# A six-sublayer decoder: order of the start, strips, experts by halves of ranks, and DVE stages as single operations

## What is computed

```
x = LN(x + attention with relative positions(x))      # a: 16 heads of 8
x = LN(x + cross attention(x, ctx))                    # b: 16 heads of 64
x = LN(x + experts(x))                                 # m, c: 7 experts of 256 slots and one that passes on
x = LN(x + gated linear attention with decay(x))       # d: 16 heads, rank 16, a norm of its own inside
x = LN(x + cross attention(x, ctx))                    # e: 16 heads of 8
x = LN(x + quantised feed-forward with a convolution(x))  # f: 512 wide, ternary weights
```

## Time and profile before

| | us |
|---|---|
| median of 3 runs | 922.15 |
| lowest and highest | 916.98, 922.53 |
| the profiled execution | 916.87 |
| its span | 915.1 |
| round of the first loop | 26.45 |
| round of the second loop | 19.59 |

### The profile page before, as it was taken

How to read it: one execution, slowest core, us unless ns; L and a number is a source line. 1 busy time by engine, 2 the same in 40 slices (tenths; PEclk the granted TensorE clock), 3 DMA queues, 4 the chain that set the end, 5 groups by cost and what they waited for, 6 DMA issues and landing times.

```text
span 915.1 us, 21252 instructions
## 1 busy us (share of the span) xinstructions
PE 753.2 (82%) x8906; PEld 552.4 (60%) x8906; DVE 565.2 (62%) x1520; ACT 402.5 (44%) x1026; POOL 215.2 (24%) x215
## 2 busy tenths in 40 slices
PE   3679999999999799999876675789888888988874
PEld 2346666767666577666665473666666665766541
DVE  0046665556666766666663733687788887788722
ACT  1345444555544455444443111354554554454521
POOL 6201111100111261111013103233333333332200
PEclk9989999999999899999988795899999999999965
DMA  8614424234443234442322110000000000000000
GB/s 338 228 47 142 142 96 139 74 119 142 141 142 130 104 98 141 141 139 102 118 88 87 52 44 20 7 8 10 14 15 11 10 11 10 14 11 4 5 4 6
DMA packets 48271, 72.16 MB, mean 79 GB/s; under 512 B 2880, under 2 KB 43328, under 8 KB 45488
## 3 DMA queue, kind: packets, MB, share of 16 engines
q1 hardware_dynamic: 45248, 63.37, 20.2%
q0 software_dynamic: 2352, 5.18, 2.5%
q10 hardware_dynamic: 576, 2.24, 0.7%
HBM read 32.32 MB, written 38.47 MB: 77 GB/s over the span
## 4 chain that ended last, share of the span: by engine, by line
PE 57%; DVE 20%; ACT 9%; issue 6%; POOL 4%; DMA 3%; POOLq 0%; SPq 0%; DVEq 0%; ACTq 0%
PE bank L466 52%; PE bank L523 4%; POOL kbd L457 3%; DVE sc L1104 2%; DVE nmxa L1108 2%; DVE sc L1111 2%; DVE nmb L1153 1%; DVE q L1412 1%; DVE scol L1399 1%; DMA row_sb<-rows 1%; ACT kbd L1048 1%; ACT kbd L1047 1%; ACT nmT L939 1%; DVE q L1148 1%; ACT kbd L1043 1%
## 5 line engine op out<-in xcount | busy, mean ns | idle before, releaser
L403 POOL TENSOR_TENSOR rext<-rext,ones 128x1008 f32<-128x1008 f32 x16 | 29.8, 1865 | 323.8 <-ACT rext L897 323.8
L949 ACT ACTIVATE pTb<-bank 77x512 f32<-77x512 f32 x128 | 66.7, 590 | 4.3 <-PE bank L466 4.3
L939 ACT ACTIVATE nmT<-bank 128x128 f32<-128x128 f32 x32 | 8.9, 278 | 125.8 <-PE bank L587 71.8
L1104 DVE TENSOR_TENSOR sc<-bank,rel 128x512 f32<-128x512 f32 x64 | 41.1, 683 | 32.4 <-PE bank L466 32.1
L1153 DVE TENSOR_REDUCE nmb<-bank 128x4 f32<-128x308 f32 x128 | 53.5, 470 | 9.8 <-PE bank L466 9.7
L1368 DVE TENSOR_TENSOR k<-bank,k_sb 128x512 f32<-128x512 f32 x64 | 41.2, 686 | 27.5 <-PE bank L466 27.2
L466 PE MATMUL bank<-wa,qa 32*128 32x512 f32 (+1 forms) x160 | 45.6, 609 | 10.4 <-ACT rext L897 6.1
L466 PE MATMUL bank<-k,xdT 128*128 128x512 f32 x96 | 50.1, 662 | 0.0
L419 POOL DMA_INDIRECT xg_dram<-x_all,to_slot x32 | 31.2, 975 | 79.8 <-DVE wpass L1262 71.0
L457 POOL TENSOR_SCALAR kbd<-kbd 128x512 f32<-128x512 f32 x16 | 30.7, 1920 | 80.1 <-ACT kbd L1043 80.1
L466 PE MATMUL bank<-nmT,k_sb 32*77 32x128 f32 x1024 | 47.6, 279 | 0.0
(11 more groups left out here) (266 smaller groups left out, 1837.3 us busy)
## 6 DMA issues: line engine op xcount, KB each, us to landing
rel_dram<-rext SPq DMA_DIRECT2D x16, 2040.0 KB, 6.4
rel<-rel_dram SPq DMA_DIRECT2D x16, 960.0 KB, 5.5
rext<-w_up SPq DMA_DIRECT2D x1, 1792.0 KB, 9.9
rel<-w_down SPq DMA_DIRECT2D x1, 1792.0 KB, 8.4
wb<-w_b SPq DMA_DIRECT2D x1, 1604.0 KB, 16.4
xT_ld<-xT SPq DMA_DIRECT2D x16, 64.0 KB, 6.3
x_all<-x ACTq DMA_DIRECT2D x1, 1024.0 KB, 10.7
wl<-w_l SPq DMA_DIRECT2D x1, 1024.0 KB, 18.2
```

Source lines behind the costliest of these rows:

```text
L949: A.activation(dst[0:C, 4 * i:4 * i + 4, :], bank[b][0:C, :].rearrange("p (a i) -> p a i", a=4), ACT.Exp).then_inc(exped["b"], 1)
L1104: added = mark(V.tensor_tensor(sc[:, part[i], :], bank[2 * j + i][:].rearrange("p (a j) -> p a j", a=4), rel[:, t % 2, part[i], :], ALU.add))
```

## The change

1. **Start.** Biases and `head8` travel with `w_a`. PE, ACT and DVE wait for these weights alone; the wait for `ld_c` moves behind the keys. The context is loaded ahead of the rows, the keys' weights ahead of the constants, `w_b` by ACT's queue, `w_l` in round 2. The keys stand behind the first relative scores, and projection and scores of sequence 1 in their midst. The right side of `rext` of sequence 0 is filled by DVE.
2. **Relative scores** are four matmuls on four strips into banks 0 to 3. `rel_last` goes to bank 2. ACT's four copies are single steps.
3. **Exponentials of a**: DVE no longer subtracts; ACT takes the exponential head by head with the maximum as bias.
4. **Cross attention b**: row sums and outputs on four strips of 32 columns. Row sums of all heads share bank 7, with one reciprocal. `c0_wo` has its rows in another order.
5. **Routing**: batches of 8, 6, 1, 1; both choices in one operation each; `to_slot` is announced first. All sends follow POOL's last fill.
6. **Experts** by halves of ranks: slots 0 to 127 of all experts first, then 128 to 255. The gather of sequence 0 needs only the first half; c, d_x, d_qk and d_gv of sequence 0 lie in the second half. The weights' ternary form, decay tables and the bias parts are computed between experts.
7. **Second loop**: single DVE operations as steps of their own in `ORDER2`; the order goes round from `e_v`. The bias is split into three bf16 rows. The inner norm has two operations for three. POOL's clamps lose the addition, which ACT's logarithm does as a bias.

```diff
-BATCHES = ((0, 8), (8, 14), (14, 16))
+BATCHES = ((0, 8), (8, 14), (14, 15), (15, 16))
...
-    "act": ("b_qlo:-1 b_nm:-1 a_e0 a_e1 a_t0 a_e2 a_e3 r_a:-2 a_t2 a_qkv:2 b_e0:-1 b_e1:-1 b_e2:-1 b_e3:-1 a_v "
-            "b_r0:-1 b_r1:-1 rel01:2 a_ln b_ln:-1 rel23:2 b_r:-1 v0 b_x").split(),
-    "pool": "rel_fill:2 r_send:-2".split(),
+    "act": ("a_e1 b_nm:-1 a_t0 a_e2 a_e3 a_t2 b_e0:-1 b_e1:-1 b_e2:-1 b_e3:-1 a_qkv:2 a_v b_rc:-1 a_ln rel0:2 "
+            "rel1:2 b_ln:-1 rel2:2 v0 rel3:2 b_r:-1 b_x b_qlo r_a:-1 a_e0:1").split(),
+    "pool": "r_send:-16 rel_fill:2".split(),
...
-                    for i in range(2):
-                        if g0 == 2:
-                            pe.wait_ge(r_mid, 4 * t + i + 1)
-                        mm(bank[3 - i][:], q[t % 3][strip(g0 + i), :], w("a0_rel")[strip(g0 + i), :]).then_inc(r_s, 1)
...
+                pe.wait_ge(a_kv, t + 1)
+                pe.wait_ge(r_lastc, t + 1)
+                need(pe, var["a"], t - 1)
+                need(pe, oT_ready["a"], t - 1)
+                need(pe, r_mid, 4 * t)
+                for i in range(4):
+                    mm(bank[i][:], q[t % 3][strip(i), :], w("a0_rel")[strip(i), :]).then_inc(r_s, 1)
...
             def b_values(j):
+
                 def f(t):
                     pe.wait_ge(exped["b"], 4 * t + 2 + 2 * j)
-                    for c in range(4):
-                        for i in range(2):
-                            last = mm(bank[5 if j else 7][half(i), c * P:(c + 1) * P], ones[0:C, 0:XH],
-                                      pTb[0:C, 8 * j + 4 * i + c, :])
-                    last.then_inc(sums["b"], 1)
...
+                    for u in range(2):
+                        for v in range(2):
+                            for s in range(4):
+                                h = 4 * (2 * j + u) + s
+                                last = mm(bank[4 if j else 6][strip(s), (2 * u + v) * P:(2 * u + v + 1) * P],
+                                          v0[0:C, h, 32 * v:32 * v + 32], pTb[0:C, at_key(h), :])
                     last.then_inc(values["b"], 1)
...
-            for t in (0, 1):
-                a_qkv_(t)
-                rel_scores(0)(t)
-                if t == 0:
-                    rel_scores(2)(t)
-                    rel_last(t)
-            rel_scores(2)(1)
+            a_qkv_(0)
+            rel_last(0)
+            rel_scores(0)
+            keys(0, 12)
+            a_qkv_(1)
+            keys(12, 14)
             rel_last(1)
-            keys()
+            rel_scores(1)
+            keys(14, 3 * XC)
+            pe.wait_ge(ld_c, 48)
...
-                    part = sc[:, 4 * i:4 * i + 4, :]
-                    A.activation(part, part, ACT.Exp).then_inc(exped["a"], 1)
+                    for h in range(4 * i, 4 * i + 4):
+                        last = A.activation(sc[:, h, :], sc[:, h, :], ACT.Exp, bias=nmxa[:, h:h + 1])
+                    last.then_inc(exped["a"], 1)
...
+            m_up_(0)
+            m_up_(1)
+            for n in range(2 * E):
+                if n + 2 < 2 * E:
+                    m_up_(n + 2)
+                m_down_(n)
+                if n == 11:
+                    d_x(0)
+                if n == 12:
+                    d_qk_(0)
+                    d_gv_(0)
+            d_rank_(0)
...
-                G.tensor_scalar(he, he, EXP_MAX, 1.0, ALU.min, ALU.add).then_inc(f_e1, 1)
+                G.tensor_scalar(he, he, EXP_MAX, None, ALU.min).then_inc(f_e1, 1)
...
-        onesrow = sb("onesrow", [32, P])
-        cbrow = sb("cbrow", [32, HID])
+        onesrow = sb("onesrow", [32, P], BF16)
+        cbrow = sb("cbrow", [32, HID], BF16)
```

More of the change, by code:

```diff
@@ L408, in rel_fill @@
                                 ones[:, 0:1].unsqueeze(2).broadcast_to(shape), ALU.mult).then_inc(r_right, 1)
+            rel_fill(0)
+            pool.wait_ge(ld_x, 16)
+            pool.wait_ge(ld_c, 48)
+            for t in range(0, B, 4):
+                G.tensor_tensor(x_all[:, t:t + 4, :], x_all[:, t:t + 4, :],
+                                row("a0_bo").unsqueeze(1).broadcast_to([P, 4, P]), ALU.add).then_inc(xb_ready["d"], 1)
+            rel_fill(1)
             def send(t):
@@ L611, in b_inj, with at_key, b_sums_, f @@
                 less_max((bank[6], bank[7], bank[4], bank[5]), turned)
+            def at_key(h):
+                return 8 * (h // 8) + 4 * (h % 2) + h % 8 // 2
+            def b_sums_(j):
+                def f(t):
+                    pe.wait_ge(exped["b"], 4 * t + 2 + 2 * j)
+                    for u in (2 * j, 2 * j + 1):
+                        for s in range(4):
+                            last = mm(bank[7][strip(s), u * P:(u + 1) * P], ones[0:C, 0:32],
+                                      pTb[0:C, at_key(4 * u + s), :])
+                    last.then_inc(sums["b"], 1)
+                return f
             def b_values(j):
@@ new lines, in _, with m_up_ @@
+            pe.wait_ge(w_sum, 1)
+            mm(bank[7][:, 0:2], ones[:], wabs[:]).then_inc(w_mean, 1)
+            def m_up_(n):
+                pe.wait_ge(m_xT_dve if n // 4 % 2 else m_xT_act, n // 8 + 1)
+                if n == 0:
+                    pe.wait_ge(ld_experts, 32)
+                need(pe, m_hid_act if n % 2 else m_hid_dve, (n - 3) // 2 + 1)
+                for c in range(HC):
+                    last = mm(bank[4 + n % 3][:, c * P:(c + 1) * P],
+                              w1e[:, n % E * HID + c * P:n % E * HID + (c + 1) * P], xgT[:, n, :])
+                last.then_inc(m_up, 1)
@@ new lines, in pass_by, with c_s0 @@
+            def pass_by(t):
+                step(V.tensor_tensor(x_all[:, t:t + 4, :], x_all[:, t:t + 4, :],
+                                     wpass[:, t:t + 4].unsqueeze(2).broadcast_to([P, 4, P]), ALU.mult))
+            def c_s0(t):
+                dve.wait_ge(ld_g[t % 3], 32 * (t // 3 + 1))
+                need(dve, normed["c"], t)
+                keep("c_s0", t, V.scalar_tensor_tensor(out=y["c"][:], in0=g[0][t % 3], scalar=gate[:, 0, t:t + 1],
+                                                       in1=x_all[:, t, :], op0=ALU.mult, op1=ALU.add))
@@ new lines, in c_s1, with d_turned, f @@
+            def c_s1(t):
+                past("c_s0", t)
+                keep("c_add", t, V.scalar_tensor_tensor(out=y["c"][:], in0=g[1][t % 3], scalar=gate[:, 1, t:t + 1],
+                                                        in1=y["c"][:], op0=ALU.mult, op1=ALU.add))
+            def d_turned(i):
+                def f(t):
+                    dve.wait_ge(d_qk, t + 1)
+                    need(dve, d_rope, t)
+                    dst, table = ((t1, "cos"), (t2, "sin"))[i]
+                    keep(f"d_r{i}", t, V.tensor_tensor(dst, bank[1][:, i * 2 * P:(i + 1) * 2 * P].rearrange(
+                        "p (a t) -> p a t", a=2), const(table).unsqueeze(1).broadcast_to([P, 2, P]), ALU.mult))
+                return f
@@ new lines, in _ @@
+            m_turn(1)
+            m_turn(3)
+            mean_sizes()
+            m_hid(1)
+            for n in range(1, 2 * E, 2):
+                if n + 2 < 2 * E and n != 11:
+                    m_hid(n + 2)
+                if n == 13:
+                    for i in range(2):
+                        d_turned(i)(0)
+                    d_rope_(0)
+                m_y(n)
+                if n < 5:
+                    ternary(n // 2)
+                if n == 5:
+                    pass_by(0)
+                    decay()
+                if n == 7:
+                    bias_parts()
+                if n == 9:
+                    c_s0(0)
+                    c_s1(0)
+                    stats_("c")(0)
+                    moments("c")(0)
+                    m_hid(13)
+                    c_norm(0)
```

645 lines of the change are left out of this document (328 added, 317 removed), and 3 rows, old and new, of the table ORDER2.

## The result

The changed kernel takes **849.36 us** (median of four runs, 846.87 to 852.15) where the kernel before takes 920.84 beside it: a ratio of 0.923, 95% interval 0.919 to 0.927. The forecast was 840, its range 815 to 866.

A forecast was written before the change was run, and what follows sets the result against it. PE's work bounds the first loop, a chain through PE and DVE the second, latency the stretch from experts to second d_x. Terms sum to -80.9 from 916.87, giving 836; 4 added makes 840 us, range 815 to 866.

The forecast's parts named there:

- Start: Up to the first attention scores: earlier first matmul and reordered loads, 36.9 us against 53.5, so -16.6.
- First round: The round without cross attention at the start of the first loop: loses DVE's subtractions, -1 us.
- Plain round of the first loop: An undisturbed first-loop round: 24.65 us instead of 26.45, with 22.4 of PE work and 2.2 of waits.
- the second rival: First loop: ACT's slower exponentials and row of copies take the gain, round 26.4 us, total 865; chance 0.2.
- 48 cross matmuls in 2.85: Cross attention's sums and outputs in the first loop: 48 matmuls on four strips take 2.85 us for 3.65, -0.8 a round.
- Fourteen rounds at -1.8: First loop: the gain of one walked round times fourteen, -25.2 us.
- Routing rounds: First loop's two routing rounds and its last: their deviation from plain rounds falls from 4.2 to 0.8 us, -3.4.
- Experts: From the experts to the second d_x: experts 1.8 us longer with handovers, d_s01(0) 3.7 behind them, net -10.4.
- Second loop: Fourteen second-loop rounds of 18.7 us instead of 19.59: -12.6, and -0.3 in the first rounds.
- in a round this gives nothing, for silu stands behind c_s0 and c_s1: Second loop: POOL's clamp with one operation instead of two gains nothing in a round.
- Drain: Draining the second loop: bias -1.4, clamp -0.6 (each twice), norm and earlier f_exp -1; -5 us, bounds -3 and -7.
- Clamp's duration: POOL's clamp in the second loop and drain: 1.3 us with one operation instead of 1.92, ends 1.0 and 1.92.

The follow-up runs named there:

- e1: The changed kernel with each load of relative scores issued only after PE's cross outputs of the round: 832.5 us, ratio 0.907.
- e4: The changed kernel with PE's queries waiting only for DVE's three reads of the ranks, the other twelve operations placed later: 842.8 us, ratio 0.915.
- e11: The changed kernel with the edits of e1, e4 and e5, and the routing batch's running sums on DVE moved behind the moments of layer a: 817.3 us, ratio 0.889.
- e5: The changed kernel with POOL's product of the convolution's weights ahead of the first gather instead of behind it: 847.4 us, ratio 0.920.
- e6: The changed kernel with POOL's clamps of two operations again and ACT's logarithms without their bias of 1: 863.5 us, ratio 0.938.

## Why the prediction was right and wrong, by its steps

The time lies in the range, 9 us from the forecast, and that is partly compensation. In the first loop plain rounds gave 11.1 us more than was booked, while the other 22.9 us stood where 0.8 had been left. Start, last scores and drain gave 6.0 more; first round and experts took 6.1 back.

- **Start: right, 2.9 better.** First matmul at 6.59 (7.5 forecast), attention scores at 34.06 (36.9). The keys took 18.9 us (18.4), what lies between them 2.5 where I gave 3.5.
- **First round: wrong by 3.** 21.43 us for 19.27. PE waits 3.45 us for the first exponentials and stands 1.09 at 50.57, with its clock at 0.76. That pause is in the trace of every variant of the changed kernel, at 1.08 to 1.09 us; no late fetch stands ahead of it, and its cause stays open.
- **Plain round of the first loop: right in kind, 0.8 better.** 22.72 of work (22.4 forecast). PE waits 0.18 for DVE's copy of q (0.2), 0.35 for the copy of v, 0.26 for xTr. The failed detail is ACT's row of copies, which I let end the round at 24.3; the wait of 0.5 before the last transposes did not come either. The exponentials stand 0.30 apart (eight in 2.45 us), as I took from the earlier trace rows, so the second rival did not come.
- **"48 cross matmuls in 2.85": right** (1.09 for the sums and 1.96 for the outputs, less the overlap). Its price was mis-sized: four strips are 1.23 a round with the reciprocal, not 0.8.
- **"Fourteen rounds at -1.8": the step that failed.** It multiplied an undisturbed round. The change makes a dense stretch of small matmuls under the relative load, and that costs 15 us in pauses and clock (e1), 16.9 by the medians, that no term had. The DMA share and the load's place were in the trace of before; I never asked what else rides on these engines.
- **Routing rounds: wrong by 6.5.** The two are 9.4 us longer than two plain ones. With the last round, which is shorter, the three deviate by 7.3 in e1 (28.85, 27.93 and 22.09), where no pauses blur it; the prediction left 0.8. PE waits 2.26 for va (275.37), as the batch's chain now stands ahead of DVE's keys and values, and 2.62 for the slots (289.19); each brings half clock behind it. I had counted fewer operations and not the 1.92 us that one of them takes beside POOL's fill (0.25 elsewhere). e4 and e11 gave most of it back: in e11 these rounds are 25.99 and 23.86.
- **Last scores to experts: right** (-6.9 for -6.4).
- **Experts: 2.9 short.** 31.1 us for 28.5; 1.76 and 0.92 of it are the waits behind the cast, and without them it was 28.5 (e5). (112 matmuls at 0.235 are 26.3 us, not the 26.5 of the forecast.) d_s01(0) started 3.9 behind them (3.7 forecast).
- **Second loop: right number, partly by luck, and one wrong reason.** 18.48 for 18.7, DVE idle 2.19 before the masks (2.2). At that the plain rounds' gain is 15.5, and rounds at the start and end of the stretch took 2.4 back where 0.3 more had been booked; 13.1 for 12.9 is the two together. But "in a round this gives nothing, for silu stands behind c_s0 and c_s1" is wrong: the clamp reaches PE through ACT's queue, and the second operation costs some 10 us in these fourteen rounds (e6).
- **Drain: -7.6, outside the bounds of -3 to -7.** Its part that hangs on the clamp is 0.4 by e6, where the sum has 1.2, so over 3 us came from pieces that it does not list or made too small; which was not tried.
- **Clamp's duration: 1.49 us**, between the value taken (1.3) and 1.92; e6 has 1.925 with two operations. The Trainium skill ("GPSIMD Engine Reference", section "Elementwise — side-by-side cycle accounting") has a loop body of up to two operations bound by its ports, by which the second would be free; here it is not, and the measurement decides.

## What to carry to other kernels

Packing small matmuls onto more strips raises the rate at which PE uses up instructions; look what the DMA engines carry in that stretch, and move a large transfer off it. A loop's forecast is its plain round times the count plus the disturbed rounds, and a wait of PE in a busy stretch has to be priced with the half clock that may follow it: here that was 6.0 us behind pauses of 8.3. For the cover of an operation follow every in-order queue that waits for it, not only the reader.

## What the runs showed of the hardware that I had not expected

- **PE's instruction fetches wait behind ordinary transfers.** One 16 KB packet came per 252 records on average; while the 960 KB load had the engines full (141.8 to 145.6), none passed, and the one at 145.83 passed as the load ended. The five fetches that came 452 to 497 records behind the one before had pauses of 1.4 to 1.8 us behind them. The Trainium skill ("Runtime: NRT & Kernel Launch", section "Instruction fetch mechanics") has 256 instructions per block of 16 KB, with which the 252 agree. It calls the cost of a block mostly hidden and PE's store 2048 instructions deep. Here PE stood still although fewer than 500 records lay between two fetches, and the cost was 15 us; the measurement decides.
- **The granted clock fell to half (1.2 GHz) behind PE waits of 1.59 us and, in two rounds of three, of 1.43; it stayed whole behind 0.99.** In e6, 0.44 us more of wait in a round cost some 10 us over fourteen rounds, of which rounds of 18.59 for 18.48 explain under 2.
- **A DVE operation between SBUF operands can last as long as POOL's beside it:** 3.88 for 0.41 us, 1.92 for 0.25, 1.97 for 0.68.
